# Row fetches in 16, 16 and 12, early turnings in one run, and a new order of tile 0 in a recommendation tower on one Trainium2 core

## The reference

```python
e = jnp.stack([tbl_0[ids[:, 0]], tbl_1[ids[:, 1]], ..., tbl_31[ids[:, 31]]], axis=1)
dots = jnp.einsum('bnd,bmd->bnm', e, e)
z = dots[:, iu, ju]                      # 496 pairs i < j
h = jnp.concatenate([z, dense_ctx], axis=1)
h = jnp.maximum(h @ W_top1 + b_top1, 0.0)    # 512 -> 512
h = jnp.maximum(h @ W_top2 + b_top2, 0.0)    # 512 -> 256
y = h @ W_top3                               # 256 -> 1
```

## Time and profile before

| | |
|---|---|
| median of 3 runs | 548.25 us (546.71 to 550.8) |
| the profiled execution | 548.03 us, of which the span from first to last instruction is 546.2 us |
| TensorE (PE) busy | 503.2 us, 92% |
| GpSimd (POOL) busy | 390.7 us, 72%, in 418 instructions |
| VectorE, ScalarE busy | 250.8 us and 184.0 us |
| granted TensorE clock, mean | 0.994 |

### The profile page before, as it was taken

How to read it: one execution, slowest core, us unless ns; L and a number is a source line. 1 busy time by engine, 2 the same in 40 slices (tenths; PEclk the granted TensorE clock), 3 DMA queues, 4 the chain that set the end, 5 groups by cost and what they waited for, 6 DMA issues and landing times.

```text
span 546.2 us, 27461 instructions
## 1 busy us (share of the span) xinstructions
PE 503.2 (92%) x11015; PEld 464.7 (85%) x11015; DVE 250.8 (46%) x592; ACT 184.0 (34%) x355; POOL 390.7 (72%) x418
## 2 busy tenths in 40 slices
PE   0765899999899999999999999999999999999997
PEld 0764799999789899998998989898899988888996
DVE  3665563543536244363625436362543536244142
ACT  1777151421505133050514215050521505142152
POOL 6777767777777777777777777777777777777710
PEclk9998999999999999999999999999999999999999
DMA  8999634444444444444444444454444444443310
GB/s 194 253 254 282 196 101 117 132 119 122 127 122 130 122 122 119 129 116 121 130 123 121 131 123 119 118 131 120 119 131 122 121 124 122 117 115 108 109 32 2
DMA packets 39173, 71.19 MB, mean 130 GB/s; under 512 B 11302, under 2 KB 25382, under 8 KB 39046
## 3 DMA queue, kind: packets, MB, share of 16 engines
q0 software_dynamic: 19728, 53.90, 35.2%
q1 hardware_dynamic: 18550, 15.14, 11.4%
q10 hardware_dynamic: 768, 0.39, 0.3%
HBM read 69.39 MB, written 0.01 MB: 127 GB/s over the span
## 4 chain that ended last, share of the span: by engine, by line
PE 60%; POOL 18%; issue 9%; DMA 7%; DVE 3%; ACT 1%; SPq 1%; DVEq 0%
PE look_ps L395 22%; POOL rows L347 18%; PE quad_ps L417 13%; PE top_ps L476 7%; PE quad_ps L379 6%; PE turn_ps L379 6%; DMA landed<-in_tbl 4%; PE top_ps L497 4%; DMA rows<-in_tbl,row_ids 2%; PE quad_ps L438 1%; DMA ids_across<-in_small_ids 1%; DVE turned L725 1%; PE top_ps L461 1%; DVE one_hot L797 1%; DVE small L787 1%
## 5 line engine op out<-in xcount | busy, mean ns | idle before, releaser
L347 POOL DMA_INDIRECT rows<-in_tbl,row_ids x411 | 390.0, 949 | 129.1 <-issue 114.1
L395 PE MATMUL look_ps<-one_hot,small 125*128 125x256 f32 (+1 forms) x1536 | 220.8, 293 | 8.6 <-DVE small L787 8.5
L395 PEld LDWEIGHTS look_ps<-one_hot,small 125*128 125x128 f32 x1536 | 195.0, 193 | 12.4 <-issue 9.9
L797 DVE TENSOR_SCALAR one_hot<-ids_across,sub_row 125x256 fp32r<-125x256 int32 (+1 forms) x384 | 118.2, 378 | 121.4 <-PE look_ps L395 112.4
L417 PE MATMUL quad_ps<-turned 128*32 128x31 f32 x7680 | 105.0, 199 | 3.5 <-issue 2.2
L417 PEld LDWEIGHTS quad_ps<-turned 128*32 128x32 f32 x7680 | 86.6, 110 | 23.8 <-issue 5.0
L570 ACT ACTIVATE ahead<-look_ps 128x512 f32<-128x512 f32 (+1 forms) x48 | 28.0, 584 | 203.5 <-PE look_ps L395 203.4
L379 PE MATMUL turn_ps<-ident,rows 128*128 128x128 f32 x418 | 62.9, 281 | 20.2 <-DMA rows<-in_tbl,row_ids 16.3
L379 PEld LDWEIGHTS turn_ps<-ident,rows 128*128 128x128 f32 x418 | 46.7, 142 | 24.8 <-issue 17.8
L379 PE MATMUL quad_ps<-ident,rows 128*128 128x128 f32 x404 | 61.1, 280 | 6.5 <-DMA rows<-in_tbl,row_ids 4.3
L561 ACT ACTIVATE turned<-turn_ps 128x512 f32<-128x512 f32 x57 | 36.1, 633 | 60.7 <-PE quad_ps L417 44.8
(11 more groups left out here) (68 smaller groups left out, 199.3 us busy)
## 6 DMA issues: line engine op xcount, KB each, us to landing
area<-in_tbl SPq DMA_DIRECT2D x640, 1.0 KB
rows<-in_tbl,row_ids POOLq DMA_INDIRECT x411
area<-in_tbl ACTq DMA_DIRECT2D x384, 1.0 KB
ids_across<-in_small_ids SPq DMA_DIRECT2D x45, 128.0 KB
landed<-in_tbl SPq DMA_DIRECT2D x6, 896.0 KB
w_sb<-in_W_top SPq DMA_DIRECT2D x4, 256.0 KB
landed<-in_tbl SPq DMA_DIRECT2D x6, 104.0 KB
w_sb<-in_W_top SPq DMA_DIRECT2D x1, 512.0 KB
```

The costliest lines, as they stand in the source:

```text
L347: pool.indirect_dma_start(out=rows[:, n % PLACES, j, :], out_offset=None, in_=tables[f], in_offset=bass.IndirectOffsetOnAxis(ap=row_ids[:, ...
L395: last = pe.matmul(look_ps[:, c * width:(c + 1) * width], small[:, f, r, part, c * P:(c + 1) * P], one_hot[n % 2][:, r, 0:width], start=(r ...
L797: last = dve.tensor_scalar(one_hot[n % 2][:, r, 0:width], ids_across[0:SP, n % IDS_RING, 0:width], sub_row[:, r:r + 1], None, ALU.is_equal)
```

## The change

It has three parts.

1. ScalarE fetches field 29 in tiles 5, 8, 11 and 14 in place of 5, 10 and 14, over three tiles in place of four, and in groups of 16, 16 and 12 (8 in the last) in place of 12, 12 and 8. There are so 410 gathers in place of 411.
2. From tile 1 on the four early turnings stand in one run behind portion 6. They stood behind portions 3, 4, 5 and 6.
3. In tile 0 the portions 0 to 3, each with an early turning behind it, come ahead of the fifth lookup, which now runs whole ahead of portion 4; the sixth stands in quarters behind portions 4 to 7. SP asks for the sixth lookup's ids ahead of the weights.

```diff
-ACT_ROW_TILES = [5, 10, 14]
+ACT_ROW_TILES = [5, 8, 11, 14]
...
-    ACT_ROW_STAGES = 4
-    ACT_ROWS = [12, 12, 8]
+    ACT_ROW_STAGES = 3
+    ACT_ROWS = [[16, 16, 12], [16, 16, 12], [16, 16, 8]]
...
-    EARLY_AFTER = [3, 4, 5, 6]
+    EARLY = 4
+    EARLY_AFTER = 6
...
+            load_ids(5)
             sp.dma_start(act_list_sb[:, :], act_list).then_inc(act_list_in, 16)
...
-            load_ids(5)
...
+            def first_look(k):
+
+                fifth, sixth = FIRST[0], FIRST[0] + 1
+                if k == PARTS // 2:
+                    look_up(fifth, 0, PRODUCTS)
+                if k > PARTS // 2:
+                    at = k - PARTS // 2 - 1
+                    look_up(sixth, PRODUCTS * at // (PARTS // 2), PRODUCTS * (at + 1) // (PARTS // 2))
...
-                    look_between(t, k)
+                    if t > 0:
+                        look_between(t, k)
+                    else:
+                        first_look(k)
...
-                    early_after = EARLY_AFTER if t > 0 else FIRST_EARLY_AFTER
-                    if k in early_after and t + 1 < TILES:
-                        turn(BEGIN[t + 1] + early_after.index(k))
-                look_between(t, PARTS)
+                    if t == 0 and k in FIRST_EARLY_AFTER:
+                        turn(BEGIN[1] + FIRST_EARLY_AFTER.index(k))
+                    if t > 0 and k == EARLY_AFTER and t + 1 < TILES:
+                        for i in range(EARLY):
+                            turn(BEGIN[t + 1] + i)
+                if t > 0:
+                    look_between(t, PARTS)
+                else:
+                    first_look(PARTS)
```

More of the change, by code:

```diff
@@ L24 @@
 TILES = BATCH // P
+ACT_LISTED = 44
+ACT_LIST_AT = [0, 44, 84]
 ACT_ROW_FIELD = FIELDS - 3
-ACT_ROW_TILES = [5, 10, 14]
+ACT_ROW_TILES = [5, 8, 11, 14]
 def pair_order():
@@ L72, in dlrm_tower @@
     ACT_ROW_UNIT = len(PAIRED) - 2
-    ACT_ROW_STAGES = 4
-    ACT_ROWS = [12, 12, 8]
+    ACT_ROW_STAGES = 3
+    ACT_ROWS = [[16, 16, 12], [16, 16, 12], [16, 16, 8]]
+    ACT_ROWS_AHEAD = [0, 44, 88]
+    LISTED = ACT_LISTED
     ROW_FIELD = FIELDS - 1
@@ L158, in dlrm_tower @@
         ident = sbuf("ident", [P, P])
-        act_list_sb = sbuf("act_list_sb", [ACT_ROW_STAGES * len(ACT_ROW_TILES), P // ACT_ROW_STAGES], int32)
+        act_list_sb = sbuf("act_list_sb", [ACT_ROW_STAGES * len(ACT_ROW_TILES), LISTED], int32)
         y_sb = sbuf("y_sb", [P, TILES])
@@ L501, in turn_all @@
             def turn_all(t):
-                for i in range(len(EARLY_AFTER), BEGIN[t + 1] - BEGIN[t]):
+                for i in range(EARLY, BEGIN[t + 1] - BEGIN[t]):
                     turn(BEGIN[t] + i)
@@ L643, in fetch_rows @@
                     return
-                stage, at = t - ACT_ROW_TILES[i] + ACT_ROW_STAGES, sum(ACT_ROWS[:chunk])
+                stage = t - ACT_ROW_TILES[i] + ACT_ROW_STAGES
+                many, at = ACT_ROWS[stage][chunk], ACT_ROWS_AHEAD[stage] + sum(ACT_ROWS[stage][:chunk])
                 if stage == 0 and chunk == 0:
@@ L651, in fetch_rows @@
                 _, numbers = nc.values_load_multi_w_load_instructions(
-                    act_list_sb[listed:listed + 1, at:at + ACT_ROWS[chunk]], engines=[mybir.EngineType.Activation],
+                    act_list_sb[listed:listed + 1, at - ACT_LIST_AT[stage]:at - ACT_LIST_AT[stage] + many], engines=[mybir.EngineType.Activation],
                     min_val=0, max_val=tables[ACT_ROW_FIELD].shape[0] - 1,
@@ L655, in fetch_rows @@
                 for k, number in enumerate(numbers):
-                    p = stage * P // ACT_ROW_STAGES + at + k
+                    p = at + k
                     act.dma_start(act_row_field[p:p + 1, :], tables[ACT_ROW_FIELD][bass.ds(number, 1), :],
@@ L699, in _ @@
                 kept = range(FIRST[t], FIRST[t + 1] - 1)
-                for chunk in range(len(ACT_ROWS)):
+                for chunk in range(len(ACT_ROWS[0])):
                     fetch_rows(t, chunk)
@@ L850 @@
     laid["row_list"] = np.ascontiguousarray(by_slot[:, FIELDS - 1].reshape(1, BATCH))
-    laid["act_list"] = np.ascontiguousarray(by_slot[:, ACT_ROW_FIELD].reshape(TILES, P)[ACT_ROW_TILES].reshape(-1, P // 4))
+    laid["act_list"] = np.ascontiguousarray(
+        np.stack([by_slot[t * P + at:t * P + at + ACT_LISTED, ACT_ROW_FIELD] for t in ACT_ROW_TILES for at in ACT_LIST_AT]))
     laid["ids"] = np.ascontiguousarray(by_slot.reshape(TILES, P, FIELDS).transpose(1, 0, 2))
```

## The result

The changed kernel takes 593.95 us (median of 4 runs, 592.33 to 597.26), the kernel before beside it on the same chip 547.6 us: a ratio of 1.084, with a 95% interval of 1.077 to 1.091. The prediction had the direction, and its range, 562 to 580, missed the time by 14 us. The profiled execution took 592.62 us with a span of 590.8 us, 44.6 us more than before, where the prediction had 22.8.

What follows compares the result with a forecast made beforehand. TensorE and POOL were taken as tied. Gated stretches 139.2, rest of tiles 3 to 13 243.4 and tile 14 20.6 make 403.2 against 380.4 us; 22.8 more on 548.03 gives 570.8, median 571.0, range 562 to 580.

Steps and rivals of the forecast that it cites:

- The gate: POOL's gather of unit 9 waits in every tile for the first early turning, 1.5 to 2.3 us from tile 4 on.
- Its rows can be turned 2.81 us after that: At unit 12, TensorE can turn the rows 2.81 us after their last gather starts on POOL.
- the second line of the table: First early turning to unit 12, summed over tiles 4 to 15: predicted 139.2 us.
- The clock falls in the new waits: Rival: TensorE drops to half speed around its new waits, giving 585 us, or 612 in all twelve tiles; chance 0.05.
- the longer piece is 2.1 us: TensorE's new waits split in two at units 11 and 12, the longer piece being 2.1 us.
- the third line of the table: Unit 12 to the next early run, summed over tiles 3 to 14: predicted 264.0 us.
- The price is 0: Tile 0's new order changes nothing at unit 12 of tile 3, counted at 142.7 for both kernels; -1 to +2 us.
- the forecast of 140.4: When the changed kernel, by the loop, would reach unit 12 of tile 3: about 140.4 us.
- the wall at 142.7: Unit 12 of tile 3 must wait for SP's rows, so it is turned at 142.7 us in both kernels.
- The 0.42: Lookup behind portion 5 waits for ScalarE's late, uncovered copy: 0.42 us a tile in tiles 3 to 13.
- The end behind unit 12 of tile 15: From unit 12 of tile 15 to the end, time is unchanged: 23.04 us.
- faster: Rival: POOL reaches unit 9 no sooner than its place is free, so the kernel takes 545.3 us; chance 0.03.

Runs made afterwards that it cites:

- no_part2: The changed kernel with its early turnings put back behind portions 3, 4, 5 and 6; 543.78 us, ratio 0.993.
- run3: The changed kernel with the run of four early turnings behind portion 3 in place of 6; 547.95 us, ratio 1.001.
- run5: The changed kernel with the run of four early turnings behind portion 5 in place of 6; 554.19 us, ratio 1.013.
- places7: The kernel before with 7 places for gathered rows in place of 9, turnings unmoved; 601.43 us, ratio 1.098.
- ids_late: The changed kernel in which, from tile 4 on, SP asks for the next lookups' ids only when unit 12 is turned; 582.51 us, ratio 1.061.
- fill: The changed kernel with 12 idle transposes on TensorE ahead of the wait of unit 12, from tile 2 on; 589.75 us, ratio 1.072.
- all3: The changed kernel with ScalarE's groups 16, 12, 16, ids asked for behind unit 12, and 12 filler transposes ahead of unit 12; 580.17 us, ratio 1.060.
- part2: The kernel before with the run of four early turnings behind portion 6 alone; 587.07 us, ratio 1.072.
- part3: The kernel before with the new order of tile 0 alone; 545.82 us, ratio 0.997.

## Why the prediction had the direction and missed the size

**The gate: right.** It sits at unit 9, opens 0.92 us after the first early turning (0.87 predicted) and POOL's 8.75 us follow. POOL stood 2.79 us beyond its usual 0.30 there in tile 4, and 1.3 to 5.8 over the twelve tiles, not 1.5 to 2.3, since the whole loop came out longer. `no_part2` shows that without it the other parts cost nothing, `run3` and `run5` show where it sets in, and `places7` that fewer places do the same without a moved turning.

**"Its rows can be turned 2.81 us after that": the step that failed most.** It measured 3.59 us on average over twelve tiles (2.92 to 5.07), 9.4 of the 10.0 us in the second line of the table. The 2.81 was read at one place out of four. At the other three that the prediction names, tiles 8, 11 and 14, the same distance was 2.81, 2.89 and 3.79 us, and the chain of waits of the kernel before showed the last:

```profile
488.43 3.75 DMA rows<-in_tbl,row_ids
```

In that tile 14 SP asks for no ids, but a 16 KB packet of the queue called instruction moves from 1.35 to 2.36 us behind the gather's start; in none of the tiles 8, 11 and 13 does one. In the changed kernel a second cause comes on top: the loop itself brings the last gather to the moment at which the features' turning releases SP's request. `ids_late` shows that this request is a cause. It isn't the only one; that the instruction packets are the other fits all four slow tiles of `ids_late` and tile 14 of before, but no run tested it. The prediction said "with rows that take 3.1 instead of 2.8 us it is 574.6", so it had the sensitivity, and too small a doubt.

The Trainium skill, "DMA: Bandwidth & Descriptors" (section on queues, rings and completion order), says that each DMA engine goes round between the queues for which it has work, a packet at a time. The trace fits it: in the seven quick tiles of `ids_late` the rows are turned 2.77 us after their gather on average, and with SP's 128 KB beside them, in the same tiles of the changed kernel, 3.47 us. The same page's fixed part and bandwidth, which the prediction weighed, give 2.3 us by estimate, and all landings measured here are longer.

**"The clock falls in the new waits": a rival I gave 0.05, and it was a part of the truth.** I computed that "the longer piece is 2.1 us". With the late landings the waits were longer, and behind tile 1 the clock fell five times: around waits of 2.68 (at unit 11 of tile 2), 2.73, 2.30, 4.12 and 2.06 us (at unit 12 of tiles 4, 7, 10 and 11), though not behind one of 2.29 (tile 5) and none of 1.98 or less. Each fall cost some 1.6 us, not the 3.4 of the rival. Four of them lie in the third line of the table and are 6.4 of its 8.5 us. `fill` and `all3`, in which that sum drops to 266.1 and 264.4, show it. I had priced the rivals one at a time; here the first error made the second one happen.

**"The price is 0" for tile 0 and tile 3: wrong by 3.4 us.** Unit 12 of tile 1 should have come 5 us earlier, at 73.3, and came 2.5 us earlier, at 75.92. TensorE in tile 0, with the unit that waits for its rows and a portion that waits for nothing visible:

```profile
48.94 0.65 PE L384 MATMUL quad_ps<-ident,rows 128*128 128x128 f32 x4 [0.89 <-DMA rows<-in_tbl,row_ids]
...
55.03 0.85 PE L422 MATMUL quad_ps<-turned 128*32 128x31 f32 x44 [2.62 <-issue]
```

I had let the new order run without a stop, and at full clock: it was granted 0.50 from 49.6 to 59.8 us, 10.2 us, where the earlier trace rows have 6.8. Unit 12 of tile 1 is 2.6 us late against the forecast; this, then the loop in tiles 2 and 3 and the fall of the clock at 111.0 bring unit 12 of tile 3 to 146.12, behind SP's rows; the forecast of 140.4 left only 2.3 us of room to the wall at 142.7. `no_part2` also shows that this wall moves: TensorE passes unit 12 of tile 3 at about 138.5 there.

**"The 0.42" for ScalarE: too small by 0.3.** The load of 16 numbers took 1.38 us and the 16 fetches 6.30 (1.3 and 6.0 predicted), so the copy is later by another 0.4 us. Half of this shows in the sum: the undisturbed tiles take 22.05 to 22.37 us against 22.13.

**The rest: right.** The end behind unit 12 of tile 15 (23.02 against 23.04), one gather less, the copy that nothing covers behind portion 5, and the way from unit 12 to the run but for the clock and ScalarE: 266.1 us in `fill`, where the clock holds, against 264.0. The reading of the other rivals held too: the gate is in every tile, and faster was never near.

## What to carry to other kernels

Moving a consumer moves the release of its buffer. Put two distances side by side: how long the consumer takes from the release to the use of the item that stands all buffers further on, and how long the producer needs for the same (release, the issues in between, landing). The price is small until the first falls below the second, and from there on each microsecond moved is lost in each round; `run5`, 10.4 us above `no_part2`, stands at that point, and the changed kernel, 50.2 above it, lies beyond. Read the landing at every place where the engine waits for it and take its spread into the sum, not one of its values.

Then ask what else the new wait does: which transfers are released by the same event and now travel with the one waited for, and whether the standing engine loses its clock. Price these on top of the loop and not as separate cases, since a longer landing makes the clock fall more likely. Filler against such a fall belongs only where the wait is sure to be longer than the filler.

## What was not expected of the hardware

- A gather's landing (its start to the turning of its rows) is not a constant: 2.73 to 2.80 us in seven tiles of `ids_late`, 3.5 to 4.0 in the four where a 16 KB packet of the instruction queue moved at the same time, and 3.6 on average, up to 5.07, in the changed kernel, where SP's 128 KB go with it.
- TensorE's granted clock fell to 0.50 around waits of 2.06 to 4.12 us in the changed kernel, but not behind one of 2.29 nor behind the 1.92 of the earlier trace rows. In `part2` it held through 2.56 us (tile 10) and fell behind 1.93 (tile 11). The length of one wait alone doesn't decide. One fall cost 1.6 us of the first layer.
- SP's five loads of row numbers between 80 and 130 us took 22.2 us before, 21.7 in `part3` and 19.0 in `no_part2`. ScalarE's fetches at the same time don't explain it by themselves: later in the same runs a load takes 2.8 to 3.5 us with them and without.
